# An expert layer on one core: how many loads of x stand in SyncE's DMA queue at once, and where the placing of matrices goes

## What is computed

```python
w = weights[conditions]                      # (32, 64, 64), one matrix for each of 32 batches
xf = einsum('bct,bcd->bdt', x, w)            # x is (32, 64, 512): 2048 tokens of 512
logits = einsum('nh,eh->ne', xf, Wr)         # 8 experts
gate = softmax(logits); top2_val, top2_idx = top_k(gate, 2)
rank = (cumsum(onehot(top2_idx)) * onehot).sum(-1); keep = rank <= cap      # cap = 640
comb = zeros((N, E)).at[tok, top2_idx].add(where(keep, top2_val, 0))
g = silu(einsum('nh,eih->eni', xf, Wg)); u = einsum('nh,eih->eni', xf, Wu)  # I = 352
out = x + einsum('ne,enh->nh', comb, einsum('eni,ehi->enh', g * u, Wd))
```

## Time and profile before

| | us |
|---|---|
| median of 3 runs | 290.49 (290.43 to 290.98) |
| the profiled execution | 289.77 |
| its span in the profile | 288.0 |
| PE busy | 270.2 (94%) |
| POOL, ACT, DVE busy | 170.1, 137.6, 136.3 |
| TensorE clock granted, mean over the span | 0.974 of full |

### The profile page before, as it was taken

The page is one execution under the profiler, slowest core; times in us unless marked ns, Lnnn a source line. Parts: engine busy times, 40 slices in busy tenths (PEclk is TensorE's granted clock), DMA queues, the critical chain, the costliest instruction groups (busy, mean ns, idle before and its releaser), DMA issues.

```text
span 288.0 us, 4133 instructions
## 1 busy us (share of the span) xinstructions
PE 270.2 (94%) x1455; PEld 211.5 (73%) x1455; DVE 136.3 (47%) x288; ACT 137.6 (48%) x242; POOL 170.1 (59%) x156
## 2 busy tenths in 40 slices
PE   8669979999999999999999999999999998999992
PEld 4445343989987888789878887777788787878981
DVE  1245894534364660675036705651563367043241
ACT  2114791325457654654456646654654565354100
POOL 5790006861177818781678278857874787685542
PEclk9959986999999999999999999999999999999999
DMA  6990598999898965795479848976894787475622
GB/s 210 374 318 3 203 366 209 356 342 341 295 287 158 276 175 86 209 242 136 68 114 267 221 75 184 239 177 101 244 212 115 117 204 113 76 82 66 183 99 88
DMA packets 26412, 54.95 MB, mean 191 GB/s; under 512 B 7280, under 2 KB 7408, under 8 KB 26288
## 3 DMA queue, kind: packets, MB, share of 16 engines
q0 software_dynamic: 10656, 22.98, 40.5%
q1 hardware_dynamic: 15728, 31.60, 32.4%
HBM read 39.56 MB, written 20.25 MB: 208 GB/s over the span
## 4 chain that ended last, share of the span: by engine, by line
PE 83%; POOL 4%; DVE 3%; issue 3%; another core or an unknown queue 2%; DMA 1%; ACT 1%; POOLq 0%
PE bank L1235 24%; PE bank L1321 20%; PE bank L1210 10%; PE bank L1327 10%; PE bank L1196 5%; PE bank L1074 2%; PE bank L1185 2%; PE bank L1334 2%; PE bank L1342 2%; PE bank L1086 2%; POOL out L503 2%; PE bank L1136 2%; POOL gate_g L471 2%; DMA xg<-xf_dram,src_row 1%
## 5 line engine op out<-in xcount | busy, mean ns | idle before, releaser
L503 POOL DMA_INDIRECT out<-y_sb,dst_row x35 | 58.1, 1661 | 32.5 <-ACT y_sb L606 23.7
L459 POOL DMA_INDIRECT xg<-xf_dram,src_row x40 | 43.8, 1095 | 52.1 <-DMA xf_dram<-xf_sb 23.2
L1321 PE MATMUL bank<-xhi,w 128*128 128x512 f32 x280 | 71.4, 397 | 0.0
L1235 PE MATMUL bank<-w,hhi 128*128 128x512 f32 x210 | 67.0, 400 | 0.0
L931 DVE TENSOR_TENSOR w<-raw,w 128x704 fp32r<-128x704 f32 (+1 forms) x35 | 37.3, 1065 | 56.0 <-ACT w L551 39.6
L1321 PEld LDWEIGHTS bank<-xhi,w 128*128 128x128 f32 x280 | 52.5, 188 | 12.6
L471 POOL DMA_INDIRECT gate_g<-gates_dram,src_row x40 | 41.6, 1041 | 12.0 <-issue 11.4
L1235 PEld LDWEIGHTS bank<-w,hhi 128*128 128x128 f32 x210 | 38.3, 188 | 7.9
L1235 PE MATMUL bank<-w,hlo 128*128 128x512 f32 x105 | 41.4, 394 | 0.0
L1327 PE MATMUL bank<-xlo,w 128*128 128x512 f32 x140 | 38.4, 396 | 0.0
L606 ACT ACTIVATE y_sb<-bank,gate_g 128x512 f32<-128x512 f32 x30 | 20.6, 687 | 33.7 <-PE bank L1235 32.2
(11 more groups left out here) (130 smaller groups left out, 291.8 us busy)
## 6 DMA issues: line engine op xcount, KB each, us to landing
raw<-wgu SPq DMA_DIRECT2D x32, 352.0 KB
x_sb<-x SPq DMA_DIRECT2D x8, 512.0 KB, 4.1
raw<-wd SPq DMA_DIRECT2D x8, 512.0 KB
xf_dram<-xf_sb SPq DMA_DIRECT2D x7, 512.0 KB, 3.3
raw<-wd SPq DMA_DIRECT2D x8, 192.0 KB
out<-x SPq DMA_DIRECT2D x1, 1280.0 KB
xg<-xf_dram,src_row POOLq DMA_INDIRECT x40
gate_g<-gates_dram,src_row POOLq DMA_INDIRECT x40
```

The source lines that it names most:

```text
L459: nc.gpsimd.indirect_dma_start(out=xg[:, n % TPE, :], out_offset=None, in_=xf_dram[:, :], in_offset=bass.IndirectOffsetOnAxis(ap=src_row[: ...
L503: nc.gpsimd.indirect_dma_start(out=out[:, :], in_=y_sb[:, n % TPE, :], in_offset=None, out_offset=bass.IndirectOffsetOnAxis(ap=dst_row[:, ...
L1235: last = nc.tensor.matmul(ps[:, :], left(c), w[:, half, part, o:o + H], start=(c == 0 and q == 0), stop=(closes and c == cs[-1] and q == 2))
L1321: nc.tensor.matmul(ACC_BANK[what][:, :], columns(what, k, part), xhi4[:, k, :], start=(k == 0 and part == 0), stop=False)
```

## The change

The loop over the loads is rewritten. Each load of x from the third on first waits for the load two before it (`X_AHEAD` is 2). Two of the placing DMAs are issued ahead of the load of pair 6, behind the wait for `wsel_in`; three more ahead of the load of pair 7, the last three behind it. Nothing else differs: the programs of PE, ACT, DVE and POOL are the same.

```diff
+X_AHEAD = 2
...
             load_x(0)
             load_x(1)
             sp.dma_start(wr_sb[:, :, :], wr[:, :, :]).then_inc(wr_in, 16)
-            for m in range(2, NM):
-                load_x(m)
-
             def place(j):
...
-            sp.wait_ge(wsel_in, 16)
-            for j in range(HALF, TT):
+
+            places = {NM - 2: (HALF, HALF + 1), NM - 1: (HALF + 2, HALF + 3, HALF + 4)}
+            for m in range(2, NM):
+                if m == NM - 2:
+                    sp.wait_ge(wsel_in, 16)
+                for j in places.get(m, ()):
+                    place(j)
+                if m >= X_AHEAD:
+                    sp.wait_ge(x_in[m - X_AHEAD], 16)
+                load_x(m)
+            for j in range(HALF + 5, TT):
                 place(j)
```

## The result

| | before | changed |
|---|---|---|
| median, us | 290.63 (290.43 to 291.32, 5 runs) | 289.45 (288.55 to 296.31, 5 runs) |
| ratio | | 0.994, 95% interval 0.9915 to 0.9965 |
| profiled execution, us | 289.77 | 289.45 |
| span, us | 288.0 | 287.7 |
| granted clock, mean | 0.974 | 0.976 |

The change is faster by 0.6%, and the forecast was 283.6. Two of the changed kernel's five runs were disturbed (293.57 and 296.31) and are not in the ratio. The profiled executions differ by only 0.3 us; where the rest of the 1.2 us between the medians comes from, no trace shows.

What follows compares the result with a forecast made beforehand. The prediction took PE's signals in the router stage, held up by a long backlog of loads in SP's DMA queue, as the bound; 290.49 - 6.9 = 283.6 us, other terms costing nothing, range 281.9 to 291.6.

Steps and rivals of the forecast that it cites:

- Where the bound was read: Router stage: 6.9 us of the chain on an unnamed piece, PE's signals arriving 2 to 6 us late.
- the end of the hole: Router stage: PE's signals flow, PE goes at its own pace, pair 7 starts at 18.6 instead of 25.53, 6.9 us gained.
- B: Rival: the hole shortens but stays; one signal held gives 286.3 us, two 289.0; chance 0.20.
- C: Rival: POOL's gathers or saturated engines hold PE's signals, not the backlog; 290.5 us, no change; chance 0.14.
- D: Rival: signals are held while loads of x land, hole ends with load 7; 291.4 or 293.9 us; chance 0.21.
- D's variant: Rival: PE itself is slow while loads write the memory it reads; same price, 0.05 of D's chance.
- E: Rival: DMA engines hardly see a shallower queue; C or D results, and their chances hold this one.
- The waits of the loads: SP's loads of x: two under way at 3.3 us each, last load 0.9 us later at 17.9, costing nothing alone.
- The dear end of 4.1 us: Loads of x at 4.1 us each: load 7 at 20.4, 3.4 us later, leaving 5.1 us gained.
- The cover of 8.5 us: Router stage: PE took pair 7 only at 25.53, so a later last load alone costs nothing.
- Placing costs nothing: SP's queue: five of eight placing DMAs move ahead of loads; they cost nothing and give nothing.
- What stands behind the stage: Logits, ranks, lists, gathers, experts: follow the router stage in a line, so the 6.9 us go through to the end.

Runs made afterwards that it cites:

- experiment 7: Kernel before with the five copies of x to out moved up between load 2 and load 3, on chip C, one run: 303.23 us.

## Why the prediction was wrong

**Where the bound was read: right, its cause wrong.** The 6.9 us of the earlier trace rows were there, and worth nearly what I said: a kernel without them takes 283 to 284.5 us on three chips (283.13, 283.63 and 284.54), the forecast was 283.6, and pair 7 starts at 18.98 where I had 18.6. But it is the kernel *before* that does this, on another chip. That the totals agree so closely is partly chance: up to pair 7 B is 6.55 us ahead of A (18.98 against 25.53), and by the mark used below 7.38. The other 0.8 us is there by the transposes ahead of the first expert's late signal (61.69 on A, 54.34 on B). That signal itself costs the end nothing: from these transposes to the mark it is 24.64 us on A and 24.61 on B. So the 1.0 us that the low end of the range took from it wasn't there to gain.

**The step that failed is "the end of the hole"**: that a long backlog in SP's queue holds PE's signals, so that with two loads under way PE would go at its own pace and pair 7 start at 18.6, 6.9 us sooner. On chip A the long backlog was gone and the hole stayed (12.38 to 16.08); pair 7 came at 25.34, 0.19 us sooner. On B and D the backlog stood in full, and no hole came. What I took as support, the late signal at the first expert, shows the same pattern: 3.1 and 3.2 us on A in both kernels, 0.43 us of ordinary waiting on B, with the same copies under way. It was never compared with anything but itself: two events of one trace had told me that the program does it, and a second chip would have told me that the program alone does not.

**The rivals.** B gives 289.0 for two signals held, near what came, and the hole is 1.8 us shorter (3.70 idle instead of 5.50). The nearness is chance: the two signals were 4.4 and 4.0 us late, not 2.7 (11.14 to 15.51 and 12.38 to 16.37), and the profiled end moved by 0.3 us. That a shorter queue shortened the hole isn't shown: one profile of each kernel, on one chip. Of C, the saturated engines alone are out as a cause on other chips (experiment 7). POOL's gathers beside the loads make no hole there either, but on chip A, where something else comes in, they are still open: the holding of the gathers was never run there. C's price rested on their being issued at the same time in both kernels, but they land sooner where fewer loads stand beside them: the last one for group 0, issued at 10.92, took 5.6 us in before on B and 4.9 in the changed kernel on C, so a hole that ends 1.1 us sooner doesn't speak against them. D's mechanism is out: load 7 was only issued at 16.31, and PE had resumed at 16.08. D's variant, that PE itself is slow and not its signals, was tested nowhere on A; on B, C and D the copies follow PE. D's slowdown came, but on the other chips and for another reason. E is out, by SP's timeline and the lower DMA share. (The last chances give C 0.13 and D 0.22 where 0.14 and 0.21 stand before; nothing hangs on it.)

**"The waits of the loads" were undersized, and their cover was the hole itself.** The term had 3.3 us for a load, from the stores of xf, which were read as not standing behind others. Seven of them were issued within 9.63 us on A, so at 3.3 us each about two were under way at a time, and still they took 3.3; why loads take longer than stores is open. Two loads under way beside gathers took 4.4 to 4.6 us (medians on B, C), so 2.2 to 2.3 us a load instead of 1.65. Load 6 was issued at 13.96 on A and 12.95 on C where I had 12.1, load 7 at 16.31 and 15.61 for 14.6. The dear end of 4.1 us was not dear enough. The cover of 8.5 us was honest for a kernel with a hole, but the sum then took the hole away, and against the kernel without it the cover was only 0.7 us (load 7 at 17.9, pair 7 at 18.6); pair 7 came 1.26 us later on C. That is the sign I had named for dearer loads: copies that follow PE at once, and pair 7 later than 19. PE's own pace needs a tile pair every 1.81 to 1.87 us, and loads at 2.2 us each can't feed it. The end shows it where no hole hides it: 2.4 us on B, 1.0 on D.

The Trainium skill (DMA: Bandwidth & Descriptors, Anatomy of one DMA) gives, by its formula for GpSimd's path, an estimated 3.2 us for such a load, near the 3.3 to 3.4 of the fastest ones here and too little for the median with two at once. Its rule of at least 1 MiB per DMA (Rules for kernel authors) does not tell these kernels apart, since the loads are 512 KB in both. What differs is how many are under way: all transfers together moved 272 GB/s in 9 to 17 us on C with two, and 357 on B with all six queued.

**"Placing costs nothing" was wrong by little.** Alone it gives 1.0048. Each issue takes SP about 0.6 us, and load 7 goes out at 14.82 instead of by 6.51.

**The clock.** I had 1.8 us for pairs at half speed in the range. On A the longer stretch below full speed took back 0.9 of the 1.1 us by which PE resumed sooner.

**What stands behind the stage: right.** From the first matmul of L1321 (L1329 in the changed kernel) to the end of the execution it is 203.44 us before and 203.40 changed on A (289.77 - 86.33 and 289.45 - 86.05), 203.62 before on B (282.57 - 78.95) and 203.46 changed on C (283.66 - 80.20). What comes ahead of that mark comes out at the end.

**What stays open**: what holds PE's signals on chip A, or whether it is PE itself that is slow there. None of 16 runs met that chip. One more trait of it is in the records. Of DMAs and their landing (the page), before on chip A:

```profile
raw<-wgu SPq DMA_DIRECT2D x32, 352.0 KB
out<-x SPq DMA_DIRECT2D x1, 1280.0 KB
xg<-xf_dram,src_row POOLq DMA_INDIRECT x40
```

and on chip B:

```profile
raw<-wgu SPq DMA_DIRECT2D x32, 352.0 KB, 4.6
out<-x SPq DMA_DIRECT2D x1, 1280.0 KB, 18.2
xg<-xf_dram,src_row POOLq DMA_INDIRECT x40, 4.4
```

The last number, the landing, is missing on A for all three. Of the eight loads of x too, A has it for the first alone (4.1 us as smallest, median and largest), so the depth of the queue can't be read there from landings. The hole and the missing records go together; that one causes the other was not tried. Nor is there a run on A without any recording: each time on record comes with a recorded clock.

## What to carry to other kernels

A wait on "remote" in a one-core kernel is a question to the chip first: run the unchanged kernel on a second one, or at least again later, before a change is aimed at it. And a cost that is covered by the very stall that a change is to remove has no cover: price it against the kernel without the stall. If loads are to be throttled, keep enough under way that latency divided by their number stays below the consumer's pace: here 4.4/2 = 2.2 us with two and 5.2/3 = 1.7 us with three, against 1.85 us a pair, so three, not two.

## What the hardware showed that I had not expected

- The same program took 290.6 us on A and 283.1, 283.6 and 284.5 on B, C and D (medians). Of the difference to B, 6.5 us are there by the first token gather (44.80 against 38.27): PE results that ACT and DVE took up 2 to 6 us late, and the half clock after them.
- On chip C a DMA share of 1.22 at 443 GB/s in 4 to 9 us, and 1.12 at 406 in the 8 us behind, delayed no signal between engines.
- A load of 512 KB took 3.3 us from issue to landing at the least. The median was 4.0 with a second load under way, 4.4 with gathers too, and 8.3 with six queued, on B. With six queued the last load was there no later than PE wanted it.
